# Values and scores on two 64-row tiles, the values' halves added in HBM, and the query's low part ahead of the turn

## What is computed

```python
q = hidden_state @ Wq + bq                      # 32 heads of 32
k = encoder_hidden_state @ Wk + bk              # 8 key heads, each shared by 4 query heads
v = encoder_hidden_state @ Wv + bv
scores = jnp.einsum('bkgld,bksd->bkgls', q, k) * scale + encoder_attention_mask
attn = jax.nn.softmax(scores, axis=-1)
out = jnp.einsum('bkgls,bksd->bkgld', attn, v)  # then out @ Wo + bo, residual, layer norm
```

## Time and profile before

| | us |
|---|---|
| median of 3 runs | 1740.94 |
| lowest and highest | 1740.63, 1742.17 |
| the profiled execution | 1740.28 |
| its span | 1738.5 |

### The profile page before, as it was taken

The page is one execution under the profiler, slowest core; times in us unless marked ns, Lnnn a source line. Parts: engine busy times, 40 slices in busy tenths (PEclk is TensorE's granted clock), DMA queues, the critical chain, the costliest instruction groups (busy, mean ns, idle before and its releaser), DMA issues.

```text
span 1738.5 us, 22384 instructions
## 1 busy us (share of the span) xinstructions
PE 1709.0 (98%) x8449; PEld 1428.8 (82%) x8449; DVE 1169.7 (67%) x1111; ACT 581.3 (33%) x669; POOL 1060.6 (61%) x587
## 2 busy tenths in 40 slices
PE   6999999999999899999999999999999999999998
PEld 6888888888888788888888877888888888888887
DVE  7999898898988656565656578446644664466443
ACT  4444354444444433333434223122312231223110
POOL 1777877877787766565766553446734673467331
PEclk9999999999999999999999999999999999999999
DMA  8443344332336577777776856556545654565432
GB/s 240 103 110 86 77 110 108 80 86 73 77 98 187 165 228 230 222 232 227 240 224 223 262 176 194 172 167 185 172 152 169 184 171 154 170 184 168 132 109 97
DMA packets 278127, 280.11 MB, mean 161 GB/s; under 512 B 62330, under 2 KB 230404, under 8 KB 278020
## 3 DMA queue, kind: packets, MB, share of 16 engines
q1 hardware_dynamic: 276672, 276.97, 52.6%
q10 hardware_dynamic: 1348, 1.71, 0.3%
HBM read 175.81 MB, written 102.76 MB: 160 GB/s over the span
## 4 chain that ended last, share of the span: by engine, by line
PE 86%; DVE 6%; POOL 3%; issue 2%; DMA 2%; ACT 1%; SPq 0%; POOLq 0%; DVEq 0%; ACTq 0%
PE ps L53 28%; PE ps L54 27%; PE ps L55 27%; PE ps L712 1%; PE ps L720 1%; POOL y L1428 1%; POOL xb L1414 1%; DMA ocr<-o_scratch 1%; POOL wqsl L1446 0%; DVE xT0r L1039 0%; DVE wq0l L1058 0%; DMA pd<-p_scratch 0%; DMA p_scratch<-prob 0%; DMA ctx<-in_ctx_dram 0%; PE ps L693 0%
## 5 line engine op out<-in xcount | busy, mean ns | idle before, releaser
L1465 POOL TENSOR_TENSOR x2Tl<-x2r,x2Th 128x1024 fp32r<-128x1024 f32 x31 | 74.5, 2404 | 275.1 <-ACT x2Th L972 275.1
L1244 DVE STREAM_TRANSPOSE x2r<-xd 128x1024 f32<-128x1024 f32 x32 | 68.8, 2150 | 200.6 <-PE ps L55 200.6
L1399 POOL TENSOR_TENSOR pr<-pr,small 128x1024 f32<-128x1024 f32 x64 | 121.9, 1904 | 97.3 <-DVE small L1132 97.2
L972 ACT CAST x2Th<-x2r 128x1024 fp32r<-128x1024 f32 x32 | 33.7, 1052 | 366.5 <-DVE x2r L1244 366.5
L1394 POOL TENSOR_TENSOR pr<-pr,small 128x1024 f32<-128x1024 f32 x64 | 121.9, 1905 | 11.3 <-DVE small L1110 9.2
L1414 POOL TENSOR_TENSOR xb<-xb,bo 128x1024 f32<-128x1024 f32 x32 | 76.9, 2402 | 71.7 <-DMA xb<-in_x_dram 71.6
L1428 POOL TENSOR_TENSOR y<-y,bet 128x1024 f32<-128x1024 f32 x31 | 74.4, 2400 | 56.9 <-DVE y L1162 56.9
L1106 DVE TENSOR_REDUCE small<-pr 128x16 f32<-128x1024 f32 x64 | 78.1, 1220 | 42.6 <-ACT pr L852 42.6
L53 PE MATMUL ps<-wo0h,oc0l 128*128 128x512 f32 x256 | 102.0, 398 | 0.0
L53 PE MATMUL ps<-wo0h,oc1l 128*128 128x512 f32 x256 | 101.6, 397 | 0.4 <-DVE y L1199 0.4
L53 PE MATMUL ps<-xT0h,wq0l 128*128 128x512 f32 x256 | 100.1, 391 | 1.1 <-DVE wq0l L1058 1.1
(11 more groups left out here) (381 smaller groups left out, 5441.9 us busy)
## 6 DMA issues: line engine op xcount, KB each, us to landing
xr<-in_x_dram SPq DMA_DIRECT2D x128, 128.0 KB, 2.9
o_scratch<-ot SPq DMA_DIRECT2D x256, 64.0 KB, 1.8
ocr<-o_scratch SPq DMA_DIRECT2D x16, 1024.0 KB, 7.7
xb<-in_x_dram SPq DMA_DIRECT2D x32, 512.0 KB, 6.6
a_scratch<-ost SPq DMA_DIRECT2D x64, 256.0 KB, 3.5
b_scratch<-ost SPq DMA_DIRECT2D x64, 256.0 KB, 6.2
xd<-x_scratch SPq DMA_DIRECT2D x128, 128.0 KB, 2.9
raw<-b_scratch SPq DMA_DIRECT2D x64, 256.0 KB, 5.8
```

What stands on the lines that cost most here:

```text
L1244: nc.vector.transpose(x2r[:].rearrange("p k (t j) -> p t k j", t=TPB), xd[:].rearrange("p t (i k) -> p t k i", k=KT)).then_inc(x2_turned, 1)
L1399: nc.gpsimd.tensor_tensor(heads(v), heads(v), mx.unsqueeze(2).to_broadcast([P, TPB * GRP, KEYS]), ALU.subtract)\
L1465: nc.gpsimd.tensor_tensor(x2T[1][:], x2r[:], f32(x2T[0][:]), ALU.subtract).then_inc(x2_lo, 1)
```

## The change

- Values (`values_of`): eight matmuls on 64 rows each, in pairs: rows 0 to 63 into `V[0]`, rows 64 to 127 into `V[1]`. The weights are `vb`'s high and low part side by side (64 columns each), so four products for each 64 rows and not three; partitions 0 to 63 of the result are the high part's, 64 to 127 the low part's. `V` is no longer doubled: values of a unit wait for the eviction of the last (`o_ev`).
- Scores: 24 matmuls on 64 rows, in pairs, of 128 columns each, which leave out the zero half of `kb`. `S` is laid out by head and no longer by m.
- Order on TensorE: query k = 0 to 5, values, scores, query k = 6, 7. Values of units 62 and 63 come behind their half tiles (slots 66, 67).
- `qs` is single. ScalarE evicts both `V` banks at once (128 x 1024) and four stores of twice the size go to `o_scratch` and `ol_scratch`; the two `turn_norm` evictions (`norm_columns`) are moved to slots 65 and 66.
- GpSimd issues, in slot 8(t+1)+5 for each block t, one accumulating DMA of 2 MB that adds `ol_scratch` onto `o_scratch`; `load_chunk` waits for it (`o_sum`).
- VectorE makes the query's low part before it turns the probabilities.
- Start: Wk, Wv and the context go with contiguous rows for each partition; the context's pieces are handed on two k at a time; Wk's low part is made by GpSimd; a small copy on ScalarE comes first; TensorE's products run by halves of k.

```diff
@@ tensor slot
-                    after(pe, o_ev, v - 1)
-                    for c in range(2):
-                        last = three(nc, V[v % 2], [vb[v % 2][:, c, x] for x in (0, 1)], [pT[v % 2][x][:, c].rearrange("p j n -> p (j n)") for x in (0, 1)],
-                                     c == 0, c == 1)
+                    after(pe, o_ev, v)
+                    for n, (c, x) in enumerate(((0, 1), (0, 0), (1, 1), (1, 0))):
+                        for h in range(2):
+                            rows = slice(64 * h, 64 * (h + 1))
+                            last = nc.tensor.matmul(V[h], vb[v % 2][rows, c].rearrange("p x a d -> p (x a d)"),
+                                                    pT[v % 2][x][rows, c].rearrange("p j n -> p (j n)"), start=n == 0, stop=n == 3)
...
-                    query(range(0, 4))
-                if 4 <= u < UNITS + 4:
+                    query(range(0, 6))
+                if 4 <= u < UNITS + 2:
                     values_of(u - 4)
-                if u < UNITS:
-                    query(range(4, 6))
...
                     for m in range(TPB):
-                        last = three(nc, S[v % 2][:, 256 * m:256 * (m + 1)], [qs[v % 2][x][:, m] for x in (0, 1)],
-                                     [kb[v % 2][:, :, x] for x in (0, 1)], True, True)
+                        for n, (x, y) in enumerate(((1, 0), (0, 1), (0, 0))):
+                            for r in range(2):
+                                rows = slice(64 * r, 64 * (r + 1))
+                                last = nc.tensor.matmul(S[v % 2].rearrange("p (j m s) -> p j m s", j=GRP, m=TPB)[:, 2 * r:2 * r + 2, m], qs[x][rows, m],
+                                                        kb[v % 2][rows, 2 * r:2 * r + 2, y], start=n == 0, stop=n == 2)
...
+                if 2 <= u - UNITS < 4:
+                    values_of(u - 4)
@@ scalar slot
-                if 4 <= u < UNITS + 4:
-                    v = u - 4
+                for v in stored_in(u):
...
-                    nc.scalar.copy(ot[v % 2][:].rearrange("p (j i m) -> p j i m", j=GRP, m=TPB),
-                                   V[v % 2].rearrange("p (j m i) -> p j i m", j=GRP, m=TPB)).then_inc(o_ev, 1)
+                    nc.scalar.copy(ot[v % 2][:].rearrange("p h (j i m) -> p (h j) i m", j=GRP, m=TPB),
+                                   VV.rearrange("p (j m i) -> p j i m", j=2 * GRP, m=TPB)).then_inc(o_ev, 1)
...
-                    after(act, scores, u - 1)
-                    nc.scalar.activation(qs[u % 2][0][:], ...
+                    after(act, scores, u)
+                    nc.scalar.activation(qs[0][:], ...
...
+                if u in (UNITS + 1, UNITS + 2):
+                    norm_columns(u - (UNITS + 1))
@@ vector slot
-                    nc.vector.tensor_tensor(p[:].rearrange("p j m s -> p m j s"),
-                                            S[v % 2].rearrange("p (m j s) -> p m j s", m=TPB, j=GRP),
-                                            mask[t % 2][:].unsqueeze(2).to_broadcast([P, TPB, GRP, KEYS]), ALU.add)\
+                    nc.vector.tensor_tensor(p[:].rearrange("p j m s -> p j (m s)"),
+                                            S[v % 2].rearrange("p (j c) -> p j c", j=GRP),
+                                            mask[t % 2][:].rearrange("p m s -> p (m s)").unsqueeze(1).to_broadcast([P, GRP, TPB * KEYS]), ALU.add)\
...
+                if u < UNITS:
+                    dve.wait_ge(q_hi, u + 1)
+                    nc.vector.scalar_tensor_tensor(out=qs[1][:], ...).then_inc(q_lo, 1)
                 if 2 <= u < UNITS + 2:
                     v = u - 2
                     dve.wait_ge(probs, v + 1)
                     after(dve, pv, v - 1)
                     nc.vector.transpose(...).then_inc(p_turned, 1)
-                if u < UNITS:
-                    dve.wait_ge(q_hi, u + 1)
-                    nc.vector.scalar_tensor_tensor(out=qs[u % 2][1][:], ...).then_inc(q_lo, 1)
@@ out_slot of vector, split_wt
+                    if f == 0 and i == 0:
+                        dve.wait_ge(o_st[1], 64 * UNITS // 2)
@@ gpsimd slot, first
+                if u >= KT + 5 and u % KT == 5 and (u - 5) // KT <= NBLK:
+                    t = (u - 5) // KT - 1
+                    for i in range(2):
+                        pool.wait_ge(o_st[i], 64 * 4 * (t + 1))
+                    after(pool, o_sum, 16 * t)
+                    nc.gpsimd.dma_start(*(d[name][t].rearrange("g p c -> (g p c)").rearrange("(q e) -> q e", q=4 * P) for name in ("o", "ol")),
+                                        accum_op=ALU.add, max_dma_last_dim=4096).then_inc(o_sum, 16)
@@ gpsimd, start
-            pool.wait_ge(kv_lo, 2)
+            for i in range(2):
+                pool.wait_ge(kv_hi, i + 1)
+                nc.gpsimd.tensor_tensor(wk[1][:, half(i)], wkr[:, half(i)], f32(wk[0][:, half(i)]), ALU.subtract).then_inc(kv_lo, 1)
```

More of the change, by code:

```diff
@@ L109, in program @@
               for i in range(2)]
-        ot = [at(f"ot{i}", 202 + 2 * i, [P, BLK]) for i in range(2)]
+        ot = [at(f"ot{i}", o, [P, 2, BLK]) for i, o in enumerate((202, 156))]
         mask = [at(f"mask{i}", 192 + i, [P, TPB, KEYS]) for i in range(2)]
@@ L326, in load_chunk @@
                 t, a = divmod(c, BLK // CHUNK)
-                for i in range(2):
-                    sp.wait_ge(o_st[i], 64 * 4 * (t + 1))
+                sp.wait_ge(o_sum, 16 * (t + 1))
                 after(sp, o_done, 4 * (c - 1))
@@ L574, in turn_ctx @@
                     for r in range(2):
[L575 to L576 removed]
+                        last = nc.tensor.transpose(C2[:, CTX * k + P * r:][:, :P],
+                                                   ctx[:, r].rearrange("p (c e) -> p c e", e=KT)[:, :, k], ident[:])
+                    if k % 2:
+                        last.then_inc(ctx_t, 1)
             def turn_norm(i):
@@ L592, in tensor @@
             nc.tensor.transpose(PJ[0][:, :KT + 2], brow[:], ident[:KT + 2, :KT + 2]).then_inc(b_turned, 1)
[L593 to L600, removed]
-            pe.wait_ge(b_done, 1)
[L602 to L608, removed]
+            for i in range(2):
+                pe.wait_ge(ctx_lo, 2 * i + 2)
+                pe.wait_ge(kv_lo, i + 1)
+                for h in range(2):
+                    for k in range(4 * i, 4 * i + 4):
+                        last = three(nc, V[h][:, :CTX], [wk[x][:, k, P * h:P * (h + 1)] for x in (0, 1)],
+                                     [ctxT[x][:, k] for x in (0, 1)], k == 0, k == KT - 1)
+                    if i:
+                        last.then_inc(k_done, 1)
+            pe.wait_ge(b_done, 1)
+            for i in range(2):
+                pe.wait_ge(kv_lo, i + 3)
+                for r in range(2):
+                    for k in range(4 * i, 4 * i + 4):
+                        last = three(nc, PJ[r], [ctxT[x][:, k, P * r:P * (r + 1)] for x in (0, 1)],
+                                     [wv[x][:, k] for x in (0, 1)], k == 0, k == KT - 1)
+                    if i:
+                        last.then_inc(v_done, 1)
             def slot(u):
@@ L1071, in vector @@
                 split_ctx(ctxT, i, i + 1)
-            for i in range(2):
-                dve.wait_ge(kv_hi, i + 1)
-                nc.vector.tensor_tensor(wk[1][:, half(i)], wkr[:, half(i)], f32(wk[0][:, half(i)]), ALU.subtract).then_inc(kv_lo, 1)
             for n in range(4):
@@ L1132, in slot @@
                     nc.vector.tensor_reduce(mx, p[:].rearrange("p j m s -> p (j m) s"), AX_X, ALU.max).then_inc(maxed, 1)
+                if u < UNITS:
+                    dve.wait_ge(q_hi, u + 1)
+                    nc.vector.scalar_tensor_tensor(out=qs[1][:], in0=Q[u % 2].rearrange("p (n m) -> p m n", m=TPB), scalar=bq[:, u % KT:u % KT + 1],
+                                                   in1=f32(qs[0][:]), op0=ALU.add, op1=ALU.subtract).then_inc(q_lo, 1)
                 if 2 <= u < UNITS + 2:
```

55 lines of the change are left out of this document (30 added, 25 removed).

## The result

| | before | after |
|---|---|---|
| median, us | 1741.2 | 1788.28 |
| lowest and highest | 1740.63, 1742.17 | 1783.83, 1791.71 |
| the profiled execution | 1740.28 | 1788.0 |

Before and after ran four times each here. The ratio is 1.0261, with a 95% interval of 1.0247 to 1.0275: 2.6% slower, 47 us where +28 was forecast. The time lies inside the range of 1742 to 1800, and 19 us past the figure.

A forecast was written before the change was run, and what follows sets the result against it. Bound: a ring over three engines, 0.05 us under TensorE's two slots. To unit 62's scores +30.8 us, end of phase -4.5, adds +3: +29.3 on 1740.28, 1769.6, said as 1769. Range 1742 to 1800.

The forecast's parts named there:

- The ring: Units 2 to 54: program-order loop over three engines bounds the phase, growing from 16.47 to 17.94 us for two slots.
- 0.63 + 0.46: VectorE's low part ahead of the turn adds 0.63 us in the slot with a turn of x, 0.46 in the other.
- the 0.38: Slot with a turn of x: ScalarE's doubled eviction delays the query's high part, adding 0.38 us with the hand-over.
- rivals 1 and 2: Units: TensorE stays the bound, 1718.7 us, chance 0.15; or the ring grows by half, 1745 to 1756 us, chance 0.10.
- TensorE's slot: TensorE's own work for one unit of the query phase: 8.03 us in place of 8.26.
- rival 4: Score pairs don't overlap at 128 columns; slot 2 us longer than before, about 1865 us; chance 0.02.
- Where TensorE waits: Units 2 to 54: TensorE idle before its scores for the low part, 1.9 us in every second slot, about 26 times.
- TensorE's clock still at 2.4 GHz: The clock stays up through the waits, as after the 1.78 us wait at 57.54 in the kernel before.
- The adds: Eight 2 MB DMAs issued by GpSimd: DMA engines have room, issue takes 1.3 us, +3 us in all (0 to 53).
- Rival 3: GpSimd's issue is long, 5 us and more a block: +25 to +50 more, 1795 to 1820 us; chance 0.07.
- The start: Wk's subtractions (2.35 us) leave VectorE for GpSimd; unit 2's scores start at about 54.7 us in place of 57.54.
- The end of the phase: The 4.25 us wait for norm columns goes and half tile 4 starts earlier: -4.5 us (ends -8 and 0).

The follow-up runs named there:

- the new start: Kernel before with only the change's start part (contiguous rows, Wk's low part on GpSimd, products by halves, small copy on ScalarE): 1743.05 us, ratio 1.0014.
- the new end: Kernel before with norm columns in slots 65 and 66 and values of units 62 and 63 behind their half tiles: 1740.33 us, ratio 0.9989.

## Why the prediction was right, and where not

- **The ring: right, and to within 1%.** 17.94 us for two slots forecast, 17.83 measured; its terms 0.63 + 0.46 measured 1.01 (17.48 - 16.47), and the 0.38 put on the doubled eviction 0.35 (17.83 - 17.48). With it rivals 1 and 2 fall. Without adds units 2 to 54 take 465.6 us where the forecast has 466.4.
- **TensorE's slot: right.** 8.03 forecast, 8.07 measured, with score pairs 0.113 us apart (0.109 forecast); with them rival 4 falls.
- **Where TensorE waits: wrong.** Forecast 1.9 us before the scores; measured 1.0 to 1.6 before the values, for the eviction, and 0.5 before the scores. The step that failed is taking the low part's consumer as the only one that feels the ring: `V` is single, so the values of a unit stand behind the eviction of the one before, which lies in the same ring. It changes the place and not the sum.
- **TensorE's clock still at 2.4 GHz: wrong.** One wait of 1.78 us was no proof; at the same place the clock fell behind 1.88 us with the new start and 1.87 with the new end, and not behind 1.85 with the low part ahead. With the ring's waits alone it fell five times between 200 and 478 us. It cost little, because a ring has slack behind a long slot.
- **The adds: wrong by a factor of five, +3 forecast and 15.7 measured.** The step that failed is "the DMA engines have room (a share of 0.39)", with only GpSimd's issue priced. The issue was priced well (1.04 for 1.3), and costs at most 1.7 us in the units. But a share over 66 us says nothing of a burst: while 2 MB run the share is 1.03 to 1.08 for 12 us (145 to 157), and loads of 16 KB land in up to 12.8 us, where they have 6 to 10 us in hand. Rival 3, a long issue, fell with its cause, and its 25 to 50 us are not what the adds cost after either; 47 is what they cost once the low part stands behind the turn (1784.6 - 1737.8). And GpSimd's issue costs about 5 us in slot 69 (507.4 - 502.7, split adds and the last one moved), where the forecast had it at nothing.
- **The start: wrong.** -2.8 forecast; -3.8 went into the sum, because 53.7 is when the low part ends and 54.7 when the scores can start. Measured +0.9 in after and -0.2 with the new start alone. The 2.35 us do leave VectorE, and the loads of x end last instead. I had named what hides the subtractions on GpSimd, but not what is late next on VectorE.
- **The end of the phase: the size near without adds, the reason in part wrong.** -4.5 forecast; after without adds is at -3.9, after at +3.1. The wait for norm columns goes, but alone it moves to the values (2.93 us). Part of the -3.9 is the clock, which the forecast didn't count: the kernel before with the low part ahead, its end unchanged, is at -3.0, with a wait of 1.81 us for the norm columns and the clock at 2.4 GHz throughout. That half tiles cover the wait for the last store holds in after (VectorE waited 3.9 us, TensorE for nothing over 0.4), but not with the adds split: in three of those kernels VectorE waits 8.6 to 8.9 us and TensorE 1.0 to 2.8 behind it. What spoils the end in after is GpSimd's issue in slot 69: the low part of `wT` came 4.8 us late.

In sum: units 2 to 62 without adds +35 (forecast +34.6), adds +16 (forecast +3), start and end about -3 without adds (forecast -8.3). So the mechanism of the ring was right, and the 19 us between forecast and result are two other terms, the adds (13) and the start and end (5). That the time still lies in the range is luck: its upper part was there for a cause that isn't at work, and the 47 us that the adds can cost were held down to 16 by the longer ring.

## What to carry to other kernels

Before an instruction is moved on an engine with gaps, look for the loop through other engines that closes over it: its own duration, less what that place waited anyway, times the turns of the loop, is what it costs. A mean DMA share is no measure of room; ask how long the largest single transfer keeps the engines, and which small load, with how little in hand, can be issued behind it; cut such a transfer to what that load can bear. And two changes that each bring little can bring much together when each hides the other, so undo both before either is called harmless.

## What the runs showed of the hardware

- An accumulating DMA from HBM to HBM issued by GpSimd: 1.04 us of GpSimd for 512 descriptors, whatever their size (4 KB or 128 bytes), and 0.82 for 128; landing after 15.6 us for 2 MB, 6.5 for 512 KB (128 descriptors), 4.0 for 64 KB (512 descriptors). While 2 MB ran, loads of 16 KB from another queue landed in up to 12.8 us (1.9 to 2.1 in the median), and SyncE's issue of two stores took 7.05 us for 1.28. The Trainium skill (DMA: Bandwidth & Descriptors, Queues, rings and completion order) has each DMA engine take the queues in turn, a packet of some 9 to 17 descriptors at a time; by that a load would wait for one packet of the add on each engine and not for the whole of it. The trace is nearer to the whole: with the first three adds of after, and of after with the low part behind, the last `vb` landed 0.2 to 1.6 us after the add.
- VectorE's subtraction with two inputs in SBUF: 1.2 us alone, 3.7 and 7.0 beside GpSimd's.
- TensorE's clock fell to 1.2 GHz five times between 200 and 478 us with the ring's waits alone, 1.2 to 1.6 us in every second slot (after, no adds), and stayed at 2.4 GHz in the kernel before with the low part ahead, whose waits there were 0.5 to 1.2 us. Where between them it turns, and on what, was not tried.
